# Second attention of a fused two-layer block: the value products of one turn in eight placed one head later

## The chip, the cores and the metric

The kernel runs on one core of a Trainium2 chip. A core has five engines that each run their own list of instructions in order and meet only at semaphores: TensorE (PE, matrix products into PSUM), VectorE (DVE), ScalarE (ACT), GpSimd (POOL) and SyncE (SP, which issues DMAs). The metric is the time of one execution on the device in microseconds; lower is better.

## What is computed

Two post-norm transformer layers over one sequence of 2048 tokens with 128 features:

```python
x = _layernorm(x + _L0_attn_ref(x, ...))   # 16 heads of 64, causal
x = _layernorm(x + _L0_ffn_ref(x, ...))
x = _layernorm(x + _L1_attn_ref(x, ...))   # 16 heads of 8, Gaussian bias on the scores
x = _layernorm(x + _L1_ffn_ref(x, ...))
```

The change lies in the second attention. Its core is

```python
scores = jnp.einsum("bhqd,bhkd->bhqk", q, k) / jnp.sqrt(jnp.float32(D))   # H = 16, D = 8
scores = scores + G              # G[q, k] = -(k - P[q])**2 * 2 / Z[q]**2, per head and query
probs = jax.nn.softmax(scores, axis=-1)
ctx = jnp.einsum("bhqk,bhkd->bhqd", probs, v)
```

over 2048 queries and 2048 keys, without a mask.

## The kernel before

The second attention is one block of the program (lines 1384 to 1660). Its work is cut into 16 **units**: four groups of four heads times four chunks of 512 queries. A unit has 8 **turns** (`TU = 8`); a turn handles, for each of the four heads `hh` of the group, two tiles of 128 keys (`j = 0, 1`, keys `at` and `at + 8` in tiles) against the unit's 512 queries. Units are counted here from 0 to 15, the turns of a unit from 0 to 7, the heads of a turn from 0 to 3. "The first head" of the change's title is `hh = 0`.

What PE does in a turn, by the names of the code:

- `scores(turn, hh)`, L1568: two products of 62 rows into one of the two halves of `ps_e`, one on rows 0 to 63 of the array and one on rows 64 to 127. It waits for the exponential two heads earlier, since `ps_e` has two buffers.
- `pv(turn, j)`, L1578, the **value products**: four products in fp32, one for each head, that add `probs` times the values onto `ps_o`. It is run for the turn before (`pv(turn - 1, ...)`). It waits for all four exponentials of that turn. The first one of a unit waits also for `s_oc` (L1576): the result of the unit before has to be copied out of `ps_o` before `ps_o` is started anew.
- `ring(op)`: the row maxima of the unit that comes next. Before a unit can be computed, the maximum of every score row has to be known (it is added to the operands as further rows). So during each unit PE computes the next unit's scores as blocks of 128 queries by 512 keys: an `x` operation makes two blocks in `ps_x`, a `y` operation one block in `ps_y` (both L1532). DVE reduces each with a maximum (L1628 for `ps_x`, L1632 for `ps_y`). `ps_x` and `ps_y` have one buffer each, so the next `x` waits until DVE has reduced the last `x`, and the next `y` for the last `y`. There are 64 blocks for each unit, 8 in a turn. Two more operations are in the same list: `fin` (L1556, four transposes of the copied result of the last unit through `ps_y`, in turn 2) and `mt` (L1550, the transpose of the maxima, in turn 7). DVE writes the transposed maxima to `maxrow` (L1637), SP moves them by DMA into `qrows`, and the first scores of the next unit wait for that DMA.

ACT runs the exponentials (L1507), four in a turn, each 128 by 1024 elements. Behind the four of turn 0 it copies the finished result of the last unit out of `ps_o` (`copy_pv`, L1513), and goes on with turn 1. DVE runs the reductions in the order in which the list has them. Neither order depends on where PE puts its value products.

The order on PE is written out by the loop in the excerpt below: in each turn the four heads' scores, one ring operation behind each, and `pv` with one more ring operation behind heads 0 and 2. `plan()` only says which ring operations belong to a turn; it isn't touched. In unit 15 no blocks are left, and the ring operations are gone but for `fin`.

Of the kernel before, what the change touches and what calls it, by code (L numbers as in the profile page):

```python
# [140 lines left out]
def build(nc, a, out):  # L141
# [15 lines left out]
    with ExitStack() as ctx:  # L157
# [82 lines left out]
        for _, kt in TURNS:  # L240
            n_add += kt > 0
            ADDED.append(n_add + (kt == 0))
# [70 lines left out]
        SCALED = {}  # L313
        BEFORE, PLAN, AFTER = plan()
        AT = {op[:2]: op[2] for op in BEFORE + [op for _, ys in PLAN for op in ys] + AFTER}

        def x_bank(g):
# [6 lines left out]
        def _(sp):  # L324
# [42 lines left out]
            for _, kind, u in sorted((n, *key) for key, n in AT.items() if key[0] in ("mt", "sum")):  # L367
                if kind == "mt":
                    place_max(u)
                else:  # L370
                    place_scale(u)
# [1010 lines left out]
    with ExitStack() as ctx:  # L1382
# [10 lines left out]
        TU = NT // 2  # L1393
# [129 lines left out]
        @block.tensor  # L1523
        def _(pe):
            def max_block(out, b):
                u, n = divmod(b, BU)
                (hh, t), k = divmod(n // NC, 4), n % NC
                j, c = k % 2, k // 2
                if n == 0:
                    pe.wait_ge(s_q[u % 3], 192 * (u // 3 + 1))  # L1530
                    pe.wait_ge(s_k[u // NQ % 2], 16 * NQ * (u // NQ // 2 + 1))
                return pe.matmul(out, qrows[64 * j:64 * j + R_M, u % 3, c, hh, t * P:(t + 1) * P],  # L1532
                                 krows[64 * j:64 * j + R_M, u // NQ % 2, hh, c * KB:(c + 1) * KB],
                                 start=True, stop=True)

            def ring(op):
                if op[0] == "x":
                    if op[3]:
                        pe.wait_ge(s_xf, op[3])
                    for i in range(op[2]):  # L1540
                        mm = max_block(ps_x[:, i, :], op[1] + i)
                    mm.then_inc(s_xp, 1)
                elif op[0] == "y":
                    if op[3]:
                        pe.wait_ge(s_yf, op[3])
                    max_block(ps_y[:, :], op[1]).then_inc(s_yp, 1)
                elif op[0] == "mt":
                    pe.wait_ge(s_mhl, op[1] + 1)
                    pe.wait_ge(s_yf, op[2])
                    pe.transpose(ps_yb[0:16 * HG, 0:P], maxhl[:, :, :, :].rearrange("p r c n -> p (r c n)"), identb[:, :])\  # L1550
                        .then_inc(s_yp, 1)
                else:
                    pe.wait_ge(s_oc, op[1] + 1)
                    pe.wait_ge(s_yf, op[2])
                    for t in range(4):
                        tr = pe.transpose(ps_y[:, t * P:(t + 1) * P], pv_raw[:, op[1] % 2, t * P:(t + 1) * P],  # L1556
                                          ident[:, :])
                    tr.then_inc(s_yp, 1)

            def scores(turn, hh):  # L1560
                u, at = divmod(turn, TU)
                e = HG * turn + hh
                if at == 0 and hh == 0:
                    pe.wait_ge(s_mrd[u % 2], 32 * (u // 2 + 1))
                if e >= 2:
                    pe.wait_ge(s_ex, e - 1)
                for j in range(2):
                    mm = pe.matmul(ps_e[:, e % 2, j], krows[64 * j:64 * j + R_END, u // NQ % 2, hh, at * P:(at + 1) * P],  # L1568
                                   qrows[64 * j:64 * j + R_END, u % 3, at * P // KB, hh, :], start=True, stop=True)
                mm.then_inc(s_st, 1)  # L1570

            def pv(turn, j):
                u, at = divmod(turn, TU)
                pe.wait_ge(s_ex, HG * turn + HG)
                if at == 0 and j == 0 and u > 0:
                    pe.wait_ge(s_oc, u)  # L1576
                for hh in range(HG):
                    mm = pe.matmul(ps_o[32 * hh:32 * hh + D1 + 1, :], v1[:, TU * j + at, HG * (u // NQ) + hh, :],  # L1578
                                   probs[:, HG * (turn % 2) + hh, j, :], start=at == 0 and j == 0,
                                   stop=at == TU - 1 and j == 1, skip_group_check=True)  # L1580
                mm.then_inc(s_pv, 1)

            pe.wait_ge(s_cv, 2)
            for op in BEFORE:
                ring(op)
            for turn, ops in enumerate(TURNS):
                rest = list(ops)
                for hh in range(HG):
                    scores(turn, hh)
                    for op in rest[:1]:  # L1590
                        ring(op)
                    rest = rest[1:]
                    if hh % 2 == 0 and turn > 0:
                        pv(turn - 1, hh // 2)
                        if len(rest) > HG - 1 - hh:
                            ring(rest[0])
                            rest = rest[1:]
                for op in rest:
                    ring(op)
            for j in range(2):  # L1600
                pv(NU * TU - 1, j)
            ring(("fin", NU - 1, Y_LAST))
# [217 lines left out]
```

## Time and profile before

| | us |
|---|---|
| median of 3 runs | 1867.43 |
| lowest, highest | 1867.12, 1868.21 |
| the profiled execution | 1867.86 |
| its span in the trace | 1865.9 |
| second attention in that span, first scores to last copy | 1104.35 to 1804.75 |
| busy over the whole span: PE, DVE, ACT, POOL | 86%, 68%, 52%, 34% |
| PE waits in the second attention put down to the copy of the result (`pv_raw`) | 15.8, in 15 waits |

The table's shares are averages over stages that differ much; GpSimd works in the first attention only. The 2 us between the execution's time and its span lie around the span. A row of the trace's timeline is a group of like instructions that follow each other: the start from the span's begin, the time that the group covers, the engine, line, operation, tiles, the count, and in brackets how long the engine was idle before it and what ended that. A row of PE that is a pair of products covers 0.38 to 0.39 us but the next product can start 0.22 us behind its start, since products are pipelined; so steps on PE are read from start to start. Overlapping rows of one engine are normal.

### The profile page before, as it was taken

What the parts mean: (1) busy time and instruction counts of PE and PEld (TensorE: products, weight loads), DVE (VectorE), ACT (ScalarE), POOL (GpSimd) and SP (SyncE); (2) the same over time, 40 slices, a digit from 0 to 9 for tenths busy, and PEclk for the clock granted to TensorE, in tenths of its full rate; (3) what the DMA queues carried; (4) which work ended last, traced back from release to release, by engine and by line L of the source; (5) the groups of instructions that cost most, each with busy time, mean ns of one, the idle gap of its engine ahead of it and who ended that gap; (6) DMA issues with size and microseconds to landing.
All of it is one profiled execution on the core that took longest, in us unless ns stands there. A gap on an engine that the chain in (4) does not pass through costs nothing. (4 is left out here: it accounts for less than half of the span.)

```text
span 1865.9 us, 27211 instructions
## 1 busy us (share of the span) xinstructions
PE 1611.7 (86%) x10416; PEld 494.4 (26%) x10416; DVE 1262.7 (68%) x2256; ACT 966.0 (52%) x1117; POOL 633.7 (34%) x354
## 2 busy tenths in 40 slices
PE   7899999999999999969998468888888888888763
PEld 3233333332333333214443111111111111111121
DVE  5767575656666666513332698888888888888626
ACT  2444444444444444423443227777777777777760
POOL 1587868778787878870000000000000000000000
PEclk8999999999999999978999669999999999999996
DMA  5000000000000000001122501112111211111000
GB/s 131 12 8 12 13 12 13 13 13 13 7 12 13 13 13 8 17 14 17 34 56 55 131 1 23 22 23 40 23 23 23 40 23 23 23 27 19 2 2 26
DMA packets 76210, 46.22 MB, mean 25 GB/s; under 512 B 22414, under 2 KB 74930, under 8 KB 76082
## 3 DMA queue, kind: packets, MB, share of 16 engines
q1 hardware_dynamic: 75266, 44.30, 11.3%
q8 instruction: 82, 1.34, 0.3%
q14 instruction: 46, 0.38, 0.1%
q10 hardware_dynamic: 816, 0.20, 0.0%
HBM read 25.53 MB, written 9.31 MB: 19 GB/s over the span
## 5 line engine op out<-in xcount | busy, mean ns | idle before, releaser
L1507 ACT ACTIVATE probs<-ps_e 128x1024 f32<-128x1024 f32 x512 | 498.6, 1022 | 241.3 <-PE ps_e L1568 240.2
L412 POOL TENSOR_TENSOR acc<-acc,probs 128x1024 f32<-128x1024 f32 (+3 forms) x256 | 503.0, 1965 | 86.8 <-ACT probs L446 66.3
L446 ACT ACTIVATE probs<-ps_e 128x1024 f32<-128x1024 f32 (+1 forms) x320 | 285.7, 901 | 381.4 <-DVE ps_e L769 134.5
L1628 DVE TENSOR_REDUCE maxpart<-ps_x 128x2 f32<-128x1024 f32 x351 | 427.8, 1219 | 54.8 <-PE ps_x L1532 52.2
L599 PE MATMUL ps_o<-probs,v 128*64 128x512 f32 (+3 forms) x1280 | 308.2, 561 | 0.2 <-ACT pv_raw L453 0.2
L1578 PE MATMUL ps_o<-probs,v 128*9 128x512 f32 x2048 | 267.5, 595 | 46.2 <-ACT probs L1507 30.4
L690 DVE TENSOR_REDUCE maxpart<-ps_x 128x2 f32<-128x1024 f32 x192 | 234.6, 1222 | 74.6 <-PE ps_x L514 74.6
L1632 DVE TENSOR_REDUCE maxpart<-ps_y 128x1 f32<-128x512 f32 x322 | 220.2, 684 | 17.9 <-PE ps_y L1532 14.8
L1532 PE MATMUL ps_x<-krows,qrows 60*128 60x512 bf16 x702 | 151.6, 400 | 88.4 <-DVE maxpart L1628 70.8
L1568 PE MATMUL ps_e<-qrows,krows 62*128 62x512 bf16 x1024 | 218.7, 381 | 9.8 <-DMA qrows<-maxrow 5.6
L693 DVE CUSTOM_DVE_ANT_0 masked<-ps_x,later 128x128 f32<-128x128 f32 (+3 forms) x256 | 115.0, 487 | 60.7 <-PE ps_x L514 59.5
L1532 PE MATMUL ps_y<-krows,qrows 60*128 60x512 bf16 x322 | 128.5, 399 | 8.1 <-DVE maxpart L1632 0.2
L514 PE MATMUL ps_x<-k_hi,q_hi 64*128 64x512 f16 (+3 forms) x640 | 112.4, 348 | 20.3 <-DVE maxpart L690 17.2
L407 POOL TENSOR_TENSOR acc<-probs 128x1024 f32<-128x1024 f32 x32 | 75.3, 2352 | 122.1 <-ACT probs L446 122.1
L564 PE MATMUL ps_e<-q_hi,k_hi 64*128 64x512 f16 (+3 forms) x640 | 115.5, 358 | 0.4 <-ACT probs L446 0.3
L564 PE MATMUL ps_e<-q_lo,k_hi 64*128 64x512 f16 (+3 forms) x640 | 112.3, 348 | 0.0
L564 PE MATMUL ps_e<-q_hi,k_lo 64*128 64x512 f16 (+3 forms) x640 | 112.2, 347 | 0.0
L1532 PEld LDWEIGHTS ps_x<-krows,qrows 60*128 60x128 bf16 x702 | 36.1, 93 | 245.8 <-DVE maxpart L1628 211.5
L599 PEld LDWEIGHTS ps_o<-probs,v 128*64 128x64 f32 x1280 | 63.7, 135 | 87.4 <-issue 78.1
L1568 PEld LDWEIGHTS ps_e<-qrows,krows 62*128 62x128 bf16 x1024 | 58.8, 95 | 102.7 <-ACT probs L1507 73.0
L564 PEld LDWEIGHTS ps_e<-q_hi,k_hi 64*128 64x128 f16 x640 | 30.8, 93 | 179.4 <-issue 116.3
L769 DVE TENSOR_TENSOR ps_e<-ps_e,ahead 128x256 f32<-128x256 f32 (+1 forms) x128 | 55.6, 443 | 25.4 <-PE ps_e L564 15.7
(246 smaller groups left out, 1400.2 us busy)
## 6 DMA issues: line engine op xcount, KB each, us to landing
qrows<-q_rows SPq DMA_DIRECT2D x64, 192.0 KB
rbc<-rden SPq DMA_DIRECT2D x128, 64.0 KB, 2.1
q_rows<-parts_q SPq DMA_DIRECT2D x24, 128.0 KB, 2.4
k_rows<-parts_k SPq DMA_DIRECT2D x24, 128.0 KB, 2.4
krows<-k_rows SPq DMA_DIRECT2D x16, 192.0 KB, 5.6
raw_h<-in_L_ffn_h_w SPq DMA_DIRECT2D x2, 1024.0 KB, 6.6
w_rows<-parts_w SPq DMA_DIRECT2D x6, 256.0 KB, 2.6
qrows<-a_rows SPq DMA_DIRECT2D x64, 24.0 KB
```

The lines of the kernel that those rows point to most:

```text
L412: pool.tensor_tensor(acc[:, u % 2, :, o:], acc[:, u % 2, :, o:], probs[:, turn % RING, :, o:], ALU.add)\
L446: act.activation(probs[:, turn % RING, :, o:], ps_e[:, turn % 2, :, o:], ACT.Exp, scale=1.0 / math.sqrt(D0))\
L564: mm = pe.matmul(out[:, h, o:], k_part["k"][rows, p % 2, keys], q_part["q"][rows, p % 2, queries], start=n == 0 and turn % 2 == 0, stop=n ...
L599: mm = pe.matmul(ps_o[D0 * h:D0 * h + D0, o:], v[:, p % 2, kt, D0 * h:D0 * h + D0], probs[:, turn % RING, h, o:], start=kt == 0, stop=kt = ...
L690: dve.reduce_max(maxpart[:, u % 2, :, t, c:c + 1], ps_x[:, :, 0:w], AX.X).then_inc(s_xf, 1)
L693: ins = dve.tensor_tensor_reduce(out=masked[:, h, 0:w], in0=ps_x[:, h, 0:w], in1=later[:, QC - w:QC], scale=1.0, scalar=-3e38, op0=ALU.add ...
L1507: act.activation(probs[:, HG * (turn % 2) + hh], ps_e[:, e % 2], ACT.Exp).then_inc(s_ex, 1)
L1532: return pe.matmul(out, qrows[64 * j:64 * j + R_M, u % 3, c, hh, t * P:(t + 1) * P], krows[64 * j:64 * j + R_M, u // NQ % 2, hh, c * KB:(c ...
L1568: mm = pe.matmul(ps_e[:, e % 2, j], krows[64 * j:64 * j + R_END, u // NQ % 2, hh, at * P:(at + 1) * P], qrows[64 * j:64 * j + R_END, u % 3 ...
L1578: mm = pe.matmul(ps_o[32 * hh:32 * hh + D1 + 1, :], v1[:, TU * j + at, HG * (u // NQ) + hh, :], probs[:, HG * (turn % 2) + hh, j, :], star ...
L1628: dve.reduce_max(maxpart[:, at:at + op[2]], ps_x[:, 0:op[2], :], AX.X).then_inc(s_xf, 1)
L1632: dve.reduce_max(maxpart[:, at:at + 1], ps_y[:, :], AX.X).then_inc(s_yf, 1)
```

## The change

One condition in PE's loop:

```diff
-                    if hh % 2 == 0 and turn > 0:
+                    late = turn % TU == 1
+                    if hh % 2 == late and turn > 0:
                         pv(turn - 1, hh // 2)
                         if len(rest) > HG - 1 - hh:
                             ring(rest[0])
                             rest = rest[1:]
```

In turn 1 of each unit the two groups of value products stand behind the scores of heads 1 and 3 and no longer behind those of heads 0 and 2. In all other turns nothing changes. Nothing is added or removed; the orders on ACT, DVE, POOL and SP are the same as before. The ring operations of the turn keep their order among themselves.

PE from turn 1's first scores to the `fin` of turn 2, in a unit between 1 and 14 (`ps_e` is scores, `ps_x` and `ps_y` the blocks for the maxima, `ps_o` value products). Before:

```order
L1568 MATMUL ps_e<-qrows,krows 128x512 x2
L1532 MATMUL ps_y<-krows,qrows 128x512
L1578 MATMUL ps_o<-probs,v 9x512 x4
L1532 MATMUL ps_x<-krows,qrows 128x512 x2
L1568 MATMUL ps_e<-qrows,krows 128x512 x2
L1532 MATMUL ps_y<-krows,qrows 128x512
L1568 MATMUL ps_e<-qrows,krows 128x512 x2
L1532 MATMUL ps_x<-krows,qrows 128x512 x2
L1578 MATMUL ps_o<-probs,v 9x512 x4
L1532 MATMUL ps_y<-krows,qrows 128x512
L1568 MATMUL ps_e<-qrows,krows 128x512 x2
L1532 MATMUL ps_x<-krows,qrows 128x512 x2
```

and now:

```order
L1568 MATMUL ps_e<-qrows,krows 128x512 x2
L1532 MATMUL ps_y<-krows,qrows 128x512
L1568 MATMUL ps_e<-qrows,krows 128x512 x2
L1532 MATMUL ps_x<-krows,qrows 128x512 x2
L1578 MATMUL ps_o<-probs,v 9x512 x4
L1532 MATMUL ps_y<-krows,qrows 128x512
L1568 MATMUL ps_e<-qrows,krows 128x512 x2
L1532 MATMUL ps_x<-krows,qrows 128x512 x2
L1568 MATMUL ps_e<-qrows,krows 128x512 x2
L1532 MATMUL ps_y<-krows,qrows 128x512
L1578 MATMUL ps_o<-probs,v 9x512 x4
L1532 MATMUL ps_x<-krows,qrows 128x512 x2
```

Each group of value products has moved behind one pair of scores and one ring operation; the next scores of turn 2 follow the last row in both.

PE at the same place in unit 15, where there are no blocks, as a piece of the difference (- before, + now):

```order
 L1578 MATMUL ps_o<-probs,v 9x512 x4
+L1568 MATMUL ps_e<-qrows,krows 128x512 x6
+L1578 MATMUL ps_o<-probs,v 9x512 x4
 L1568 MATMUL ps_e<-qrows,krows 128x512 x4
 L1578 MATMUL ps_o<-probs,v 9x512 x4
-L1568 MATMUL ps_e<-qrows,krows 128x512 x4
-L1578 MATMUL ps_o<-probs,v 9x512 x4
-L1568 MATMUL ps_e<-qrows,krows 128x512 x4
+L1568 MATMUL ps_e<-qrows,krows 128x512 x2
 L1556 MATMUL ps_y<-ident,pv_raw 128x128 x4
```

The first row is the last value products of turn 0. Behind it came four products of scores (head 3 of turn 0, head 0 of turn 1), and now come six, with head 1 of turn 1.

## Rows read from the trace of the kernel before

**Rows 1.** Busy time by stretch: units 1 to 14, then turn 2 of unit 7.

```profile
core 0: us, PE busy (x) PEld busy (x) DVE busy (x) ACT busy (x) POOL busy (x), PEclk, DMA share, GB/s
1150.00:1766.00 616.00, 510.28 (x3627) 111.64 (x3626) 545.12 (x665) 439.79 (x461) 0.00 (x0) 1.00 0.14 24
...
1423.52:1429.33 5.81, 4.92 (x38) 1.29 (x36) 5.23 (x8) 3.87 (x5) 0.00 (x0) 1.00 0.00 0
```

**Rows 2.** Waits of PE, 1104 to 1806: total us, times, longest.

```profile
PE ps_o L1578 <- ACT pv_raw L1513: 15.8, 15, 1.1
```

**Rows 3.** Timeline of PE, unit 7, turn 1 to the start of turn 2.

```profile
1417.23 0.38 PE L1568 MATMUL ps_e<-qrows,krows 62*128 62x512 bf16 x2
...
1418.87 1.04 PE L1578 MATMUL ps_o<-probs,v 128*9 128x512 f32 x8 [1.05 <-ACT pv_raw L1513]
1419.85 0.39 PE L1532 MATMUL ps_x<-krows,qrows 60*128 60x512 bf16 x2
1420.08 0.38 PE L1568 MATMUL ps_e<-qrows,krows 62*128 62x512 bf16 x2
...
1421.57 0.39 PE L1532 MATMUL ps_x<-krows,qrows 60*128 60x512 bf16 x2 [0.67 <-DVE maxpart L1628]
1421.88 1.05 PE L1578 MATMUL ps_o<-probs,v 128*9 128x512 f32 x8
1422.86 0.39 PE L1532 MATMUL ps_y<-krows,qrows 60*128 60x512 bf16 x1
...
1423.52 0.38 PE L1568 MATMUL ps_e<-qrows,krows 62*128 62x512 bf16 x2
1424.12 0.63 PE L1556 MATMUL ps_y<-ident,pv_raw 128*128 128x128 f32 x4 [0.22 <-DVE maxpart L1632]
1424.68 0.62 PE L1578 MATMUL ps_o<-probs,v 128*9 128x512 f32 x4
```

**Rows 4.** Timeline of ACT at the same place.

```profile
1417.22 1.02 ACT L1507 ACTIVATE probs<-ps_e 128x1024 f32<-128x1024 f32 x1 [0.31 <-PE ps_e L1568]
1418.14 0.59 ACT L1513 ACTIVATE pv_raw<-ps_o 128x512 f32<-128x512 f32 x1
1418.61 1.03 ACT L1507 ACTIVATE probs<-ps_e 128x1024 f32<-128x1024 f32 x1
1420.50 1.94 ACT L1507 ACTIVATE probs<-ps_e 128x1024 f32<-128x1024 f32 x2 [0.86 <-PE ps_e L1568]
```

**Rows 5.** Timeline of DVE at the same place.

```profile
1417.44 1.23 DVE L1628 TENSOR_REDUCE maxpart<-ps_x 128x2 f32<-128x1024 f32 x1 [0.28 <-PE ps_x L1532]
1418.58 0.68 DVE L1632 TENSOR_REDUCE maxpart<-ps_y 128x1 f32<-128x512 f32 x1
1420.28 1.22 DVE L1628 TENSOR_REDUCE maxpart<-ps_x 128x2 f32<-128x1024 f32 x1 [1.03 <-PE ps_x L1532]
1421.42 0.68 DVE L1632 TENSOR_REDUCE maxpart<-ps_y 128x1 f32<-128x512 f32 x1
1422.02 1.21 DVE L1628 TENSOR_REDUCE maxpart<-ps_x 128x2 f32<-128x1024 f32 x1
1423.29 0.69 DVE L1632 TENSOR_REDUCE maxpart<-ps_y 128x1 f32<-128x512 f32 x1
```

**Rows 6.** Timeline of PE, first scores of units 7 and 8.

```profile
1412.74 0.39 PE L1568 MATMUL ps_e<-qrows,krows 62*128 62x512 bf16 x2 [0.47 <-DMA qrows<-maxrow]
...
1456.98 0.39 PE L1568 MATMUL ps_e<-qrows,krows 62*128 62x512 bf16 x2 [0.44 <-DMA qrows<-maxrow]
```

**Rows 7.** Timeline of PE, first value products in turns 1 and 2 of unit 0.

```profile
1109.86 1.05 PE L1578 MATMUL ps_o<-probs,v 128*9 128x512 f32 x8
...
1114.82 0.62 PE L1578 MATMUL ps_o<-probs,v 128*9 128x512 f32 x4 [0.47 <-ACT probs L1507]
```

**Rows 8.** Timeline of PE, unit 15: value products of turn 1, scores of turn 2.

```profile
1771.95 1.05 PE L1578 MATMUL ps_o<-probs,v 128*9 128x512 f32 x8 [1.11 <-ACT pv_raw L1513]
...
1775.36 0.39 PE L1568 MATMUL ps_e<-qrows,krows 62*128 62x512 bf16 x2 [0.52 <-ACT probs L1507]
```

## The prediction

> **What bounds the kernel now.** The change touches one stage, so I read that stage first by stretches, then PE's waits there, then the timelines of PE, ACT and DVE around one copy of a result. In units 1 to 14 no engine is full: in 616.00 us DVE is busy 545.12 (88%), ACT 439.79 (71%), and PE's 510.28 are pipelined records that say little [rows 1]. PE's granted clock is 1.00 in the stretch, the 2.4 GHz level. A unit takes 1456.98 - 1412.74 = 44.24 us [rows 6], 5.53 a turn. What sets it is a chain through PE's fixed order: PE stands at an operation that waits, and everything behind it stands too, the block that DVE needs next and the scores that ACT needs next.
>
> Turn 1 is the longest of a unit, 1423.52 - 1417.23 = 6.29 us [rows 3]; turn 2 takes 5.81 [rows 1]. The reason stands in rows 3 and 4. The exponentials of turn 0 end at 1418.24, ACT copies the last unit's result from 1418.14 to 1418.73, and the first value products of the turn start at 1418.87, 0.14 behind the copy's end. PE had reached them at 1417.23 + 2 x 0.22 = 1417.67 (scores, then a `y` block, 0.22 us each from start to start, as 1419.85 to 1420.08 shows [rows 3]). So PE stands 1.20 us. Behind it in the queue stand the next `x` block, for which DVE has been free since about 1419.2 and starts at 1420.28 after 1.03 us without work [rows 5], and the scores of head 1, for which ACT then waits 0.86 us [rows 4]. The profile counts 15 such waits with 15.8 us [rows 2], one for each of the units 1 to 15.
>
> **The change part by part.** Nothing is added or removed on any engine, and no wait is new: the value products keep their two waits (exponentials of the turn before, copy) and only come later. The question is what PE does in the 1.20 us, and what comes late for it. I lay the new order out on unit 7 with the durations of rows 3 to 5. Steps: PE goes on 0.22 us behind scores or a block, 0.31 from a block to value products (1421.57 to 1421.88), 0.98 from value products to the next (1418.87 to 1419.85) [rows 3]. DVE and ACT start 0.42 to 0.43 behind the product that they need (1419.85 to 1420.28, 1420.08 to 1420.50) [rows 3 to 5]. DVE's next reduction starts 1.14 us behind an `x` one and 0.60 behind a `y` one, and its end releases PE 0.07 later (1421.50, then 1421.57) [rows 3, 5]. ACT's next exponential starts 0.92 behind the last (1.94 - 1.02) [rows 4].
>
> 1. Scores of turn 1 head 0 at 1417.23 and the `y` block: unchanged.
> 2. Scores of head 1 need the last exponential of turn 0, which ends at 1418.24 [rows 4]: 1418.30 (before 1420.08).
> 3. `x` block needs the `x` reduction that ends at 1418.67 [rows 5]: 1418.74 (before 1419.85). DVE takes it up at 1419.18, right behind its `y` reduction of 1418.58. Its hole of 1.03 us is closed.
> 4. First value products: 0.31 behind the block is 1419.05. The copy would have let them go at 1418.87, so the wait for the copy is gone and they run 0.18 later than before. They end PE's step at 1420.03.
> 5. `y` block 1420.03; scores of head 2 beside it, since the exponential they need ended at 1419.64 [rows 4].
> 6. `x` block: DVE's `x` reduction runs from 1419.18 for 1.22, to 1420.40: 1420.47 (before 1421.57).
> 7. Scores of head 3: they need the exponential of head 1, which can now start 0.92 behind the 1418.61 one, 1419.53, and ends at 1420.55: 1420.69.
> 8. `y` block: its reduction before starts at 1420.46 and takes 0.68: 1421.21. Second value products 0.31 later, 1421.52 (before 1421.88).
> 9. `x` block 1422.50, scores of turn 2 head 0 at 1422.73 (before 1423.52: 0.79 earlier). Turn 1 takes 5.50.
> 10. `fin` needs DVE's last `y` reduction: the `x` one starts at 1421.06, the `y` one 1.14 later at 1422.20 and ends at 1422.88; with the 0.14 that rows 3 and 5 show for it (1423.98 to 1424.12) that is 1423.02, or 0.32 behind the scores, 1423.05. Value products 0.56 behind it: 1423.61, before 1424.68. Here the two orders are the same again, 1.07 us earlier; the `x` block behind it comes as much earlier and finds DVE free.
>
> What has to be ready by then is ready: the last exponential of turn 1 starts at about 1421.6 and ends at 1422.6, one microsecond ahead of the value products at 1423.61. From step 10 on every operation of all engines has the order of before, so the rest of the unit shifts as a whole, and with it the last maxima, their DMA and the scores of the next unit, which wait for that DMA [rows 6]. I take 1.05 us for a unit, since step 9's 0.79 and DVE's 1.1 pull either way by little: 14 x 1.05 = 14.7 us for units 1 to 14.
>
> Unit 0 has no result to copy. Its first value products of turn 1 stood free at 1109.86 [rows 7]; they now come behind one scores step (0.22) and a `y` block that may wait for its reduction, together 0.2 to 0.8 later. Those of turn 2 waited 0.47 for an exponential [rows 7], which hides most: 0 to 0.35 us lost, taken as 0.2. Unit 15 has the wait for the copy too, 1.11 us [rows 8], but no blocks to fill it, only the scores of head 1. The scores of turn 2 waited 0.52 for an exponential there [rows 8], and ACT sets the pace; what its earlier start can give is 0 to 0.52, taken as 0.4.
>
> Sum: -14.7 + 0.2 - 0.4 = -14.9 us. The profiled execution took 1867.86, 0.43 more than the median; against the median that makes 1867.43 - 14.9 = 1852.5. The bounds for a unit: at most the whole stand of 1.20 us goes (17.0 in all, 1850.4), at least step 9's 0.79 with a further 0.04 lost to DVE (10.5, 1856.9).
>
> DVE has by far the highest busy share of the stage, yet it is idle 1.03 us exactly where PE stands [rows 5]. The Trainium skill, page Perfetto Trace Analysis, section Identifying the Most-Contended Engine, says to take the engine of highest occupancy and optimize that one first; taken by itself it would make this change worth nothing, since DVE's work stays as it is, against the sum above. The row speaks for the sum, so I keep the rule as a rival.
>
> **The rivals.** (A) *DVE sets the pace after all, and the time comes back.* If the other turns were run at DVE's rate, an earlier start would only let it wait elsewhere. A pair of `x` and `y` takes 1.74 us and a turn has 8/3 pairs, 4.64 us, against turns of 5.53 on average: DVE could follow. Against it also: the idle time in rows 5. Result: no change in units 1 to 14, 1867.2. The rule of the Trainium skill's page Perfetto Trace Analysis, named above, would give the same.
>
> (B) *DVE half a microsecond late.* In steps 3, 6 and 8 PE now goes exactly when a reduction ends, in place of the copy. Had DVE at step 3 half a microsecond more of work, each of the steps would be as much later and half of the gain would stay: 14 x 0.5 = 7, so 1860.2. Rows 5 show DVE on time in unit 7, and the waits for the copy are 15 with 1.1 at most, near alike; so not likely.
>
> (C) *Slower.* The second value products (L1578) now stand behind a `y` block that waits for DVE, and right ahead of turn 2. If DVE is a whole pair behind there, 1.74 us, step 8 comes at 1422.95, all behind it 1.74 later than in my list, and the unit loses 1.74 - 1.05 = 0.69: 14 x 0.69 = 9.7, so 1877. It decides from 1.05 us of lateness on. For it: the new order makes three blocks in the turn depend on a reduction's end. Against it: ACT's copy and DVE read different PSUM tiles, and DVE's 0.60 and 1.14 hold in each row.
>
> That the change does nothing is excluded: the order on PE shows the move in every unit.
>
> **How the numbers follow.** A difference of 0.2% (3.7 us) is about what a measurement of this kernel can tell from no change. The forecast, 1850.4 to 1856.9, gets 0.79; (A) 0.09; (B) 0.07; (C) 0.05. The range of 8 in 10 takes in the bounds of the forecast and a little beyond: 1849.5 to 1858. Faster by over 0.2%: forecast and (B), 0.86. Within: (A), 0.09. Slower: (C), 0.05.
>
> **What would show it.** Right: no wait of PE for `pv_raw` but the one of unit 15; turn 1 at 5.5 us for 6.29 and turn 2 at 5.5 for 5.81; the unit at 43.2 us for 44.24; DVE without the hole of 1.03; turns 3 to 7 as before. Wrong: turn 1 shorter and the first scores of the next unit no earlier (A), waits of PE for reductions in turn 1 that grow by half a microsecond or more (B, C), or a lower granted clock in the stage.

## The result and the profile after

The changed kernel takes 1852.69 us (median of 6 runs, 1851.69 to 1853.84), against 1868.3 us for the kernel before in the same comparison (6 runs, 1867.12 to 1869.08). The ratio is 0.9918, 95% interval 0.9905 to 0.993. The forecast was 1852.5 us in a range of 1849.5 to 1858. The span of the profiled execution went from 1865.9 to 1850.5 us. Of these 15.4 us, 15.36 lie in the stage itself: from its first scores to its last value products it is 699.14 us before and 683.79 now.

Waits of PE in the second attention after the change: line, what it waited for, total us, times, longest.

```profile
PE ps_x L1532 <- DVE maxpart L1629: 44.9, 77, 0.7
PE ps_o L1578 <- ACT probs L1507: 29.9, 81, 1.4
PE ps_e L1568 <- ACT probs L1507: 11.2, 23, 0.6
...
PE ps_o L1578 <- ACT pv_raw L1513: 0.2, 1, 0.2
```

The 15 waits for the copy of a result with 15.8 us [rows 2] have become one of 0.2 us, in unit 15. A new wait has come in: scores wait for exponentials 23 times, 11.2 us, 15 more than the 8 (4.3 us) of the kernel before. It is the wait of the second scores in the changed turn, [0.47] in the next timeline. PE in unit 7, from the scores that open turn 1 to the first value products of turn 2, to be laid beside rows 3:

```profile
1410.05 0.38 PE L1568 MATMUL ps_e<-qrows,krows 62*128 62x512 bf16 x2
1410.27 0.38 PE L1532 MATMUL ps_y<-krows,qrows 60*128 60x512 bf16 x1
1411.12 0.39 PE L1568 MATMUL ps_e<-qrows,krows 62*128 62x512 bf16 x2 [0.47 <-ACT probs L1507]
1411.54 0.39 PE L1532 MATMUL ps_x<-krows,qrows 60*128 60x512 bf16 x2
1411.86 1.05 PE L1578 MATMUL ps_o<-probs,v 128*9 128x512 f32 x8
1412.83 0.39 PE L1532 MATMUL ps_y<-krows,qrows 60*128 60x512 bf16 x1
1412.84 0.60 PE L1568 MATMUL ps_e<-qrows,krows 62*128 62x512 bf16 x2
1413.27 0.39 PE L1532 MATMUL ps_x<-krows,qrows 60*128 60x512 bf16 x2
1413.49 0.38 PE L1568 MATMUL ps_e<-qrows,krows 62*128 62x512 bf16 x2
1414.01 0.39 PE L1532 MATMUL ps_y<-krows,qrows 60*128 60x512 bf16 x1
1414.32 1.05 PE L1578 MATMUL ps_o<-probs,v 128*9 128x512 f32 x8
1415.30 0.39 PE L1532 MATMUL ps_x<-krows,qrows 60*128 60x512 bf16 x2
1415.53 0.38 PE L1568 MATMUL ps_e<-qrows,krows 62*128 62x512 bf16 x2
1415.84 0.66 PE L1556 MATMUL ps_y<-ident,pv_raw 128*128 128x128 f32 x4
1416.43 0.62 PE L1578 MATMUL ps_o<-probs,v 128*9 128x512 f32 x4
```

From the opening scores to the first value products it is 1.81 us (before 1418.87 - 1417.23 = 1.64), but now a pair of scores and an `x` block are issued in that time. From the opening scores to the `fin` it is 5.79 us (6.89 before), to the value products behind it 6.38 (7.45): 1.07 us earlier. ACT and DVE at the same place, beside rows 4 and 5:

```profile
1410.04 1.02 ACT L1507 ACTIVATE probs<-ps_e 128x1024 f32<-128x1024 f32 x1 [0.31 <-PE ps_e L1568]
1410.96 0.59 ACT L1513 ACTIVATE pv_raw<-ps_o 128x512 f32<-128x512 f32 x1
1411.43 3.98 ACT L1507 ACTIVATE probs<-ps_e 128x1024 f32<-128x1024 f32 x4
```

```profile
1410.26 1.22 DVE L1629 TENSOR_REDUCE maxpart<-ps_x 128x2 f32<-128x1024 f32 x1 [0.27 <-PE ps_x L1532]
1411.40 0.68 DVE L1633 TENSOR_REDUCE maxpart<-ps_y 128x1 f32<-128x512 f32 x1
1411.99 1.21 DVE L1629 TENSOR_REDUCE maxpart<-ps_x 128x2 f32<-128x1024 f32 x1
1413.26 0.69 DVE L1633 TENSOR_REDUCE maxpart<-ps_y 128x1 f32<-128x512 f32 x1
```

The hole of 1.03 us on DVE and the one of 0.86 us on ACT are gone; all four exponentials of turn 1 run as one chain behind the copy. The stretches of the two turns and the distance from unit 7 to unit 8:

```profile
1410.05:1415.53 5.48, 4.85 (x36) 1.03 (x33) 5.22 (x6) 5.27 (x6) 0.00 (x0) 1.00 0.16 35
1415.53:1421.07 5.54, 4.87 (x38) 1.29 (x36) 5.01 (x8) 2.97 (x4) 0.00 (x0) 1.00 0.00 0
```

```profile
1405.52 0.39 PE L1568 MATMUL ps_e<-qrows,krows 62*128 62x512 bf16 x2 [0.43 <-DMA qrows<-maxrow]
...
1448.67 0.39 PE L1568 MATMUL ps_e<-qrows,krows 62*128 62x512 bf16 x2 [0.39 <-DMA qrows<-maxrow]
```

The columns of the first are those of rows 1: length, then busy time of PE, PE's weight loads, DVE, ACT and POOL, and the granted clock, 1.00 as before, the DMA share and GB/s. Turn 1 takes 5.48 us (6.29), turn 2 5.54 (5.81), the unit 43.15 (44.24).

### The profile page after: what moved, and what is told of

It is laid out like the page before. It is cut to its first block and busy times, and to the rows that moved or that the text cites. A ratio compares the mean times of both kernels' runs of the same rounds, so it can differ in the third digit from the quotient of the medians.

```text
span 1850.5 us, 27211 instructions
## 1 busy us (share of the span) xinstructions
PE 1616.8 (87%) x10416; PEld 496.9 (27%) x10416; DVE 1261.2 (68%) x2256; ACT 966.4 (52%) x1117; POOL 634.1 (34%) x354
## 2 busy tenths in 40 slices
DMA packets 76210, 46.22 MB, mean 25 GB/s; under 512 B 22414, under 2 KB 74930, under 8 KB 76082
## 3 DMA queue, kind: packets, MB, share of 16 engines
q1 hardware_dynamic: 75266, 44.30, 11.2%
## 5 line engine op out<-in xcount | busy, mean ns | idle before, releaser
L1568 PE MATMUL ps_e<-qrows,krows 62*128 62x512 bf16 x1024 | 218.1, 382 | 16.8 <-ACT probs L1507 11.2
```

## The experiments

Eight more kernels ran. For each I give the time, its ratio to the kernel before as measured beside it (1868.3 us for the change, 1868.07 for turn3_only, first_only and the two with half a copy, 1868.06 for the others), and the length of the turns of unit 7, read from start to start of the turns' first scores in the trace. Over units 1 to 14 turns 1 to 6 repeat within 0.01 us and turns 0 and 7 within 0.15 (0.29 in the late orders), so the lengths of turns 1 to 4 tell more than the total. For the first seven rows of the table the turns 5 and 6 are within 0.01 us of before, turn 7 within 0.06 and turn 0 within 0.11, which is inside their own scatter.

| kernel | us | ratio, 95% interval | turn 1 | turn 2 | turn 3 | turn 4 | unit 7 |
|---|---|---|---|---|---|---|---|
| before | 1868.3 | 1 | 6.29 | 5.81 | 5.29 | 5.18 | 44.24 |
| the change | 1852.69 | 0.9918, 0.9905 to 0.993 | 5.48 | 5.54 | 5.29 | 5.17 | 43.15 |
| turn3_only | 1857.03 | 0.9938, 0.9923 to 0.9953 | 6.29 | 5.81 | 5.41 | 4.43 | 43.53 |
| first_only | 1851.79 | 0.9912, 0.9897 to 0.9926 | 5.31 | 5.67 | 5.29 | 5.17 | 43.17 |
| half_copy_before | 1868.02 | 0.9998, 0.9989 to 1.0008 | 6.08 | 5.81 | 5.28 | 5.17 | 44.01 |
| half_copy_after | 1855.98 | 0.9933, 0.9916 to 0.995 | 5.48 | 5.54 | 5.29 | 5.17 | 43.17 |
| tiny_copy_before | 1864.29 | 0.9979, 0.997 to 0.9989 | 5.87 | 5.81 | 5.29 | 5.18 | 43.86 |
| all_late | 1816.63 | 0.9724, 0.9708 to 0.974 | 4.64 | 5.48 | 5.26 | 4.96 | 41.24 |
| late_but_1 | 1831.53 | 0.9804, 0.9789 to 0.9818 | 5.53 | 5.64 | 5.26 | 4.96 | 42.17 |
| best8 | 1806.68 | 0.9672, 0.9658 to 0.9687 | 4.48 | 5.47 | 5.13 | 4.96 | 40.34 |

(For the last three kernels turns 0, 5, 6 and 7 differ from before too.)

### Does it need the copy? turn3_only

```diff
-                    late = turn % TU == 1
+                    late = turn % TU == 3
```

> The value products of turn 3 of each unit stand behind heads 1 and 3; turn 1 is as in the kernel before. No copy of a result is near turn 3. Theory A (the gain is the wait for the copy, filled with other work): turn 3 has no such wait, so nothing is gained; as in unit 0 turn 3 gets about 0.7 us longer and turn 4 about 0.5 shorter, the time is that of before or up to 3 us more (1868 to 1871). Theory B (the later place is better in itself: in any turn the first value products stand at the exponentials of the turn before and hold the next scores and the next block up behind them): laid out with the steps of the prediction, turn 3 gets 0.1 longer and turn 4 some 0.7 shorter, since the value products then find their exponentials done; 0.65 a unit, about 10 us less (1858).

Measured: 1857.03 us, 11 less than before. In turn 3 there is no copy, and still turn 3 with turn 4 takes 9.84 us for 10.47. Theory A, by which only the wait for the copy can be gained, falls; B's numbers came in (5.41 and 4.43 for 5.4 and 4.5). How much of the gain in turn 1 is the copy, this run doesn't say; the next ones do. The place where it gains is the first value products of turn 4. In the kernel before, PE in turn 4 of unit 7:

```profile
1435.06 0.38 PE L1532 MATMUL ps_x<-krows,qrows 60*128 60x512 bf16 x1
1435.90 1.05 PE L1578 MATMUL ps_o<-probs,v 128*9 128x512 f32 x8 [0.46 <-ACT probs L1507]
```

and with the move in turn 3:

```profile
1429.92 0.39 PE L1568 MATMUL ps_e<-qrows,krows 62*128 62x512 bf16 x2
1430.15 0.38 PE L1532 MATMUL ps_x<-krows,qrows 60*128 60x512 bf16 x2
1430.46 1.04 PE L1578 MATMUL ps_o<-probs,v 128*9 128x512 f32 x8
```

The value products of turn 4 need the last exponential of turn 3. With the late order the scores of turn 3's heads come one group of value products earlier in the turn, so its exponentials are done when PE gets to turn 4, and the 0.46 us of idle time there are gone.

### How much of the stand is the copy? half_copy and tiny_copy

```diff
-                act.activation(pv_raw[:, u % 2], ps_o[:, :], ACT.Copy).then_inc(s_oc, 1)
+                act.activation(pv_raw[:, u % 2, 0:QC // 2], ps_o[:, 0:QC // 2], ACT.Copy).then_inc(s_oc, 1)
...
+            dve.memset(pv_raw[:, :, :], 1.0).then_inc(s_cv, 1)
```

and `0:8` for `0:QC // 2` in tiny_copy_before. PE and ACT wait for the memset at the start of the stage, by a wait that the edit adds (`act.wait_ge(s_cv, 3)` on ACT). These three kernels leave out part of the result.

> The order of before; ACT's copy of the result takes only the first 256 of 512 columns, the other half of pv_raw holds ones set once, so half of each unit's result is left out. The copy gets some 0.2 us shorter. Theory A: PE's stand in turn 1 gets as much shorter, 0.2 us for each of 15 units, 3 us in all (1865). Theory B's place of the products does not bear on it. If the copy were not what PE waits for: 1868.

> The changed order with the same half copy. If the value products no longer wait for the copy, as step 4 of the prediction says (0.18 us behind it), a shorter copy gives nothing: within 1 us of the change (1852 to 1853). If the copy still holds them up: 3 us less.

> The order of before; ACT copies only 8 of the 512 columns of the result, the rest of pv_raw holds ones set once, so nearly all of each unit's result is left out. The copy takes about 0.2 us for 0.59. Theory A (all of the stand is the copy): turn 1 loses nearly the whole gain of the change by itself, 6.29 to about 5.5 us. Theory C (two waits of the value products add up in the stand: the last exponential of turn 0 holds them until 1418.29 in unit 7's time, the copy for 0.58 us beyond that): only the copy's part above the exponential can go, 0.40 us, so turn 1 takes 5.89 and stays 0.41 above the change's 5.48; 14 to 15 units make 6 us less than before.

The copy takes 0.38 us with 256 columns and 0.17 with 8, for 0.59. Turn 1 in the old order follows it one to one: 6.29, 6.08, 5.87, and no other turn changes. In the changed order half a copy changes nothing, 5.48 as before. So step 4 of the prediction is shown: the changed order doesn't wait for the copy. And theory C is right: 0.42 us of the stand went with the part of the copy that could be taken away here, and reckoned to the end of the exponential the copy's share is 0.58. What remains of the stand is the wait for the exponential. Even with the tiny copy turn 1 stays 0.39 us above the change's and turn 2 keeps its 5.81, so the copy's wait is at most a little over half of the 1.07 us that the change gains in the two turns.

The totals missed, half_copy_before and half_copy_after by 3 us and tiny_copy_before by 2. The turns of units 1 to 15 came in (3.2 us less in sum for half_copy_before, 6.3 for tiny_copy_before); the rest was lost in unit 0, which takes 46.22, 46.05 and 46.23 us in these three, for 42.69 before and 42.87 with the change. Two things make up the 3.5 us of half_copy_before, 0.86 in turn 0 and 2.67 in turn 1. The first is a side effect of the edit (turn 0 takes 4.93 us for 4.07). ACT loads its table for the exponentials once before them; before, and with half a copy:

```profile
1055.29 1.28 ACT L1507 ACT_TABLE_LOAD   x1 [8.43 <-PEq L842]
1105.69 1.28 ACT L1509 ACT_TABLE_LOAD   x1 [58.91 <-PE ps_e L1570]
```

In the kernel before this load of 1.28 us lies 49 us ahead of the first scores and costs nothing. With the added wait on ACT in front it comes only when the first scores are done, and PE stands 0.95 us at the third scores. The second is TensorE's clock, in turn 1 (8.01, 8.37 and 8.02 us for 5.34 before and 6.03 with the change). The stretch from 1106 to 1116 us, before and with half a copy (the last numbers are granted clock, DMA share, GB/s):

```profile
1106.00:1116.00 10.00, 8.54 (x55) 1.71 (x55) 9.35 (x11) 7.80 (x9) 0.00 (x0) 0.93 0.01 2
```

```profile
1106.00:1116.00 10.00, 8.57 (x37) 1.39 (x38) 7.49 (x9) 6.99 (x8) 0.00 (x0) 0.50 0.01 2
```

From 1060 to 1102, where PE has only the first unit's blocks to compute and is idle 0.7 to 0.9 us in front of most `x` blocks, the granted clock is 0.50, the 1.2 GHz level. It rises to 2.4 GHz once the scores have come in, in the kernel before between 1107 and 1108, in these three kernels not by 1116. But the memset, the table load and the shorter copy are not what a late rise needs. Here are the kernel before and first_only, which has none of them:

```profile
1110.00:1112.00 2.00, 1.89 (x15) 0.23 (x7) 1.95 (x4) 0.58 (x2) 0.00 (x0) 1.00 0.03 8
```

```profile
1110.00:1112.00 2.00, 2.00 (x11) 0.13 (x8) 1.71 (x2) 1.02 (x1) 0.00 (x0) 0.50 0.04 8
```

The lists of before, the change, turn3_only, first_only and the three kernels with other orders below are the same up to turn 1 of unit 0. In three of the seven traces the granted clock from 1104 to 1112 is 0.78 to 0.84, and in four (first_only, all_late, late_but_1, best8) it is 0.50, with 7.04 to 7.78 us for turn 1 of unit 0. So the rise comes at different moments behind the same work. Whether it differs between executions of one kernel no trace here shows, since one was kept of each, and whether the edits of the three copy kernels move it further is open.

### Which of the two moves? first_only

```diff
-                    late = turn % TU == 1
-                    if hh % 2 == late and turn > 0:
-                        pv(turn - 1, hh // 2)
+                    places = (1, 2) if turn % TU == 1 else (0, 2)
+                    if hh in places and turn > 0:
+                        pv(turn - 1, places.index(hh))
```

> Turn 1 has its first value products behind head 1, as in the change, and its second ones behind head 2, one place earlier than in the change and as in the kernel before. Both theories: moving the first ones is what gains. Laid out with the steps of the prediction turn 1 becomes 5.3 us (5.5 in the change) and turn 2 5.6, so 1.1 to 1.2 us a unit, 1 to 2 us less than the change in all (1851). If the move of the second ones carried part of the gain, this would be 1855 or more.

Turn 1 takes 5.31 and turn 2 5.67, together 10.98 us against 11.02 with both moved: the same unit length within 0.04 us. Over units 1 to 14 the mean is 43.11 us, for 43.15 with both. The move of the first value products carries the gain; that of the second adds nothing (1851.79 against 1852.69 us, and 0.04 us a unit the other way). The move puts two things in front of the value products, a pair of scores for ACT and a block for DVE. Which of them pays was not tested. In unit 15, where there are no blocks, turn 1 of the change is 0.36 us shorter by the scores alone.

### All turns late, and a mixed order

all_late has `hh % 2 == 1` in every turn, late_but_1 `late = turn % TU != 1`, which undoes the change inside that order. best8 gives each turn its own two heads:

```diff
-                    if hh % 2 == 0 and turn > 0:
-                        pv(turn - 1, hh // 2)
-                        if len(rest) > HG - 1 - hh:
-                            ring(rest[0])
-                            rest = rest[1:]
+                    places = ((2, 3), (1, 2), (1, 2), (2, 3), (1, 3), (1, 3), (0, 3), (1, 2))[turn % TU]
+                    for j in range(2):
+                        if hh == places[j] and turn > 0:
+                            pv(turn - 1, j)
+                            if len(rest) > HG - 1 - hh:
+                                ring(rest[0])
+                                rest = rest[1:]
```

> The value products of every turn stand behind heads 1 and 3. Theory B (value products held up by exponentials are better placed a head later wherever that is so): every turn gains what its two stands cost, the average turn goes from 5.53 us to about 5.1, with DVE's work of 4.64 a turn as floor; laid out with the steps of the prediction a unit takes 40.6 us, 50 us less than before in all (1818), 35 less than the change. Theory A' (the change gains mostly because turn 1 alone differs from the turns around it, so that two close or two distant groups of value products meet at its ends): with all turns alike that is gone, 1850 or more.

> All turns but turn 1 have their value products behind heads 1 and 3; turn 1, where the copy is, has them behind heads 0 and 2. This undoes the change inside the all-late order. Theory B with the copy's own part: turn 1 and 2 lose 0.8 to 0.9 us a unit against all turns late, 13 us (1831). If the copy matters little, the loss is that of any other turn, 0.3 us a unit, 5 us (1823).

> The places of the two groups of value products by turn 0 to 7 are (2,3), (1,2), (1,2), (2,3), (1,3), (1,3), (0,3), (1,2), each the head behind whose scores they stand. Theory B: what counts is that the products come when their exponentials are done and DVE has its next block in time; laid out with the steps of the prediction this order takes 40.1 to 40.3 us a unit, 56 us less than before (1812), 6 less than all turns late.

Theory A' falls. B's totals came in near for the first two, 1816.63 for 1818 and 1831.53 for 1831; best8 took 1806.68 for 1812. For all_late that is partly luck: a unit was to take 40.6 us and takes 41.01 on the mean of units 1 to 14 (41.24 in unit 7), so these units gave 45 us and not 51, and unit 15, which has no blocks, gave another 4.8. For best8 the unit came in, 40.29 for 40.1 to 40.3, and unit 15 gave 3.0 more. late_but_1 against all_late is the change once more, among other neighbours: turns 1 and 2 take 11.17 us for 10.12, and a unit 42.05 for 41.01, 1.04 more on the mean of units 1 to 14, where 0.8 to 0.9 was expected. In all it is 14.9 us, near the 15.6 of the change itself. The largest of PE's waits, 1150 to 1740, in all_late and then in best8:

```profile
PE ps_x L1532 <- DVE maxpart L1628: 47.3, 83, 0.7
...
PE ps_o L1578 <- ACT pv_raw L1513: 0.2, 1, 0.2
```

```profile
PE ps_x L1532 <- DVE maxpart L1630: 20.1, 55, 0.5
PE ps_e L1568 <- ACT probs L1507: 7.3, 27, 0.9
```

In that stretch the kernel before has 65 waits of value products for exponentials with 22.5 us; in these two kernels PE's list has none. Not all such holding back is gone in best8: the weight loads of its value products still wait 13.3 us for exponentials, for 73.1 before. Busy time of best8 from 1150 to 1670, columns as in rows 1:

```profile
1150.00:1670.00 520.00, 484.16 (x3374) 99.59 (x3371) 502.17 (x621) 407.21 (x425) 0.00 (x0) 1.00 0.16 28
```

DVE is busy 502.17 of 520 us, 97%, for 462.54 (89%) in the kernel before. Its idle time there, 17.83 of 520 us, is an estimate of the most that a better order of PE's list could still take out of this stretch, since no order takes a reduction away; whether one takes it was not tested. best8 beats the kernel before by 3.3% and the change by 2.5%.

## Why the prediction was right, and where it wasn't

**The replay on unit 7.** By the prediction's own steps, with the start of turn 1's scores as zero: scores of head 1 at 1.07 (predicted 1.07), `x` block 1.49 (1.51), first value products 1.81 (1.82), second `x` block 3.22 (3.24), scores of head 3 at 3.44 (3.46), `y` block 3.96 (3.98), second value products 4.27 (4.29), scores of turn 2 at 5.48 (5.50), `fin` 5.79 (5.82), value products 6.38 (6.38). Each start came within 0.03 us of its forecast, so the waits were the forecast ones.

**The gain of a unit.** Steps 9 and 10 gave 1.07 us, I took 1.05 as a middle. Measured is 44.24 - 43.15 = 1.09 in unit 7, and 15.16 us in units 1 to 14 together, for 14.7. Turns 3 to 6 kept their lengths and turn 7 its own within 0.05 us, so the shift was carried whole through the unit and over the DMA of the maxima to the next one: rival (A) is out. It was worked out on one unit, and held because the other 13 are alike: units 1 to 13 take 44.20 to 44.34 us before and 43.15 to 43.23 now, unit 14 takes 43.72 and 42.62.

**Unit 0 and unit 15.** Unit 0 was to lose 0.2; it went from 42.69 to 42.87 us, turn 1 longer by 0.69, turn 2 shorter by 0.53. That this fits is luck in part: the prediction said nothing of the clock's rise in this unit, which in the two traces happens to lie ahead of turn 1, and where it comes later, as in first_only, unit 0 takes 44.59 us. Unit 15 was to gain 0.4; its turn 1 went from 4.90 to 4.54.

**The sum.** -14.9 us predicted, -15.6 measured on the medians, -15.4 between the two spans. By parts it is -15.16 for -14.7 (units 1 to 14), +0.18 for +0.2 (unit 0) and -0.38 for -0.4 (unit 15).

**The rule of the busiest engine.** The Trainium skill, page Perfetto Trace Analysis, section Identifying the Most-Contended Engine, says to optimize the engine of highest occupancy first. The prediction took this to mean that only less work on DVE can pay, which is its own reading. So read, the traces don't bear it out: DVE was at 88% with holes of 1.03 us behind a PE that stood, and the change and best8 gained without taking a single reduction away. What they took away is DVE's idle time. In best8, at 97% busy, little of that is left; no run here takes work off DVE.

**What the prediction had wrong is the name of the stand.** It put all 1.20 us down to the copy, by the profile's "15 waits, 15.8 us, pv_raw". Of these the exponential would have held the value products for 0.62 us in any case, since it ended at 1418.24 and let them go at 1418.29, and PE had got there at 1417.67 by the prediction's count; the copy added 0.58. The count itself is 0.09 too early: it takes 0.22 us from the `y` block to the value products where the prediction's own step is 0.31. So PE got there at 1417.76, the stand is 1.11 us and not 1.20, and the exponential's part 0.53. This touches the upper bound of the gain (14 x 1.11, near 15.7 in all for 17.0) and not the forecast; the lower bound of 10.5 leaves out units 0 and 15, which the upper one counts in. The replay came out right all the same, since step 2 used the exponential's end and not the copy's for what moves ahead. The wrong name hid what the experiments found: the same move pays in turns without any copy, and in all turns together it pays more than three times as much. That it doesn't pay in unit 0 fits: there the value products of turn 1 started at 1109.86 [rows 7], 0.32 us behind the `x` block at 1109.54, and waited for nothing on ACT.

Rivals (B) and (C) needed DVE late by 0.5 or 1.74 us. DVE's reductions start at the times of the replay within 0.03 us, so nothing of them showed.

## What to carry to other kernels

On an engine that works in order, look for the operation that stands while other engines have holes, and put in front of it what they wait for; busy shares don't show this, a timeline of one period on three engines does. In the profile a wait for two things is put down to the later one alone, so before a wait is called by a name, work out how long it would last without it. A schedule of this kind that repeats can be laid out by hand from the starts in the trace, and the place that pays in one turn should be tried in all of them. When an experiment adds a wait, look at what else moves behind it: here it was a table load.

## What the runs showed of the hardware

With the steps taken from one unit (0.22 us between products of 512 columns in bf16, 0.31 ahead of and 0.98 behind a group of four fp32 value products, 0.42 from a product's start to the reader's, 0.92 and 1.14 from one exponential or reduction to the next), the starts of a new order could be foretold within 0.03 us in the turn where it changed. I had not expected that much regularity. Over whole units it was less regular: with every turn late the unit was foretold at 40.6 us and took 41.0.

I had also not expected that the moment at which TensorE's clock rises in unit 0 would differ so much. With the same lists up to turn 1 of unit 0, the granted clock from 1104 to 1112 is 0.78 in the kernel before and 0.50 in first_only, and unit 0 takes 42.69 and 44.59 us. In the kernels with a shorter copy it takes 46.05 to 46.23, of which 0.86 us lie in turn 0, with the table load of 1.28 us that an added wait moved in front of the first exponential. Such shifts are as large as some of the effects under test, and only the lengths of the later turns kept them apart.
